# Layer 1's projections, attention and routed low-rank part as one program

## The reference

```
x = x + tanh(g_xattn[1]) * attention1(layernorm(x), ctx, Wq, Wk, Wv, Wo)     # 16 heads of 96, 4 key heads
x = x + tanh(g_ffn[1])   * lora1(layernorm(x), A, B, Wr, br)

def lora1(x, A, B, Wr, br):                       # 8 experts, rank 16
    scores = 8 * softmax(x @ Wr.T + br)           # (token, 8)
    low = einsum('bsd,hrd->bshr', x, A)           # (token, 8, 16) = 128 columns
    return 2 * einsum('bshr,hor,bsh->bso', low, B, scores)
```

## Time and profile before

| | |
|---|---|
| median of 3 runs | 2810.8 us (2809.34 to 2810.83) |
| the profiled execution, time / span | 2811.97 us / 2810.2 us |
| PE busy | 2734.7 us (97% of the span), 13880 matmuls |
| DVE, ACT, POOL busy | 1142.7, 1064.0, 664.0 us |
| granted TensorE clock, mean | 0.985 |
| stretches with PE idle of over 2 us at a time | 2371 to 2389 us and 2740 to 2764 us, and some in layer 0 |

### The profile page before, as it was taken

One profiled execution on the slowest core, in us unless ns is written; L12 is line 12 of the kernel. 1 busy time (PEld: TensorE's weight loads), 2 busy tenths in 40 slices (PEclk: granted clock), 3 DMA queues, 4 the chain that ended last, 5 costly groups with the idle time before them and its releaser, 6 DMA issues. The chain is left out here.

```text
span 2810.2 us, 37299 instructions
## 1 busy us (share of the span) xinstructions
PE 2734.7 (97%) x13880; PEld 2319.6 (83%) x13880; DVE 1142.7 (41%) x2147; ACT 1064.0 (38%) x2405; POOL 664.0 (24%) x611
## 2 busy tenths in 40 slices
PE   8999999999999998999999999999999998999997
PEld 6888888878788886888888888879899897788885
DVE  3111111122233333755666566535321010877755
ACT  4222222222233335755555555424223111755523
POOL 3000000000111112755555555403000000544410
PEclk9999999999999999999999999999999998999998
DMA  6333333332523233533333333244224221433302
GB/s 232 113 113 113 112 110 110 107 104 105 202 90 103 91 104 125 160 102 105 107 107 102 105 108 107 70 167 126 78 85 148 69 89 63 121 87 81 88 21 68
DMA packets 299883, 302.21 MB, mean 108 GB/s; under 512 B 124688, under 2 KB 252424, under 8 KB 291768
## 3 DMA queue, kind: packets, MB, share of 16 engines
q1 hardware_dynamic: 298616, 297.73, 33.7%
q10 hardware_dynamic: 1088, 2.10, 0.2%
HBM read 199.34 MB, written 100.42 MB: 107 GB/s over the span
## 5 line engine op out<-in xcount | busy, mean ns | idle before, releaser
L45 PE MATMUL pb<-p_w,p_xt 128*128 128x512 f32 (+1 forms) x992 | 397.4, 401 | 2.7 <-DVE p_w L737 2.2
L47 PE MATMUL pb<-p_w,p_xt 128*128 128x512 f32 (+1 forms) x992 | 388.9, 392 | 0.0
L46 PE MATMUL pb<-p_w,p_xt 128*128 128x512 f32 (+1 forms) x992 | 387.7, 391 | 0.0
L522 POOL TENSOR_TENSOR p_w<-p_raw,p_w 128x512 fp32r<-128x512 f32 x48 | 68.4, 1434 | 966.7 <-ACT p_w L637 966.5
L1154 ACT ACTIVATE at_p<-pb,at_nmax 112x487 f32<-112x487 f32 x256 | 171.2, 670 | 327.6 <-DVE at_nmax L1229 327.6
L745 DVE TENSOR_REDUCE p_inv<-p_sq 128x4 f32<-128x512 f32 (+1 forms) x62 | 42.6, 686 | 472.9 <-ACT p_sq L644 472.9
L45 PEld LDWEIGHTS pb<-p_w,p_xt 128*128 128x128 f32 (+1 forms) x992 | 185.4, 187 | 43.1 <-DVE p_w L737 3.1
L47 PEld LDWEIGHTS pb<-p_w,p_xt 128*128 128x128 f32 (+1 forms) x992 | 185.1, 187 | 42.5
L46 PEld LDWEIGHTS pb<-p_w,p_xt 128*128 128x128 f32 (+1 forms) x992 | 185.7, 187 | 38.2
L999 POOL TENSOR_TENSOR at_k<-at_kr,at_k 128x488 fp32r<-128x488 f32 (+1 forms) x94 | 116.2, 1236 | 365.5 <-DVE at_k L1243 365.5
L1248 DVE TENSOR_TENSOR at_ptlo<-pb,at_pthi 125x448 fp32r<-125x448 f32 (+1 forms) x256 | 148.0, 620 | 84.9 <-ACT at_pthi L1176 84.9
(11 more groups left out here) (251 smaller groups left out, 6255.1 us busy)
## 6 DMA issues: line engine op xcount, KB each, us to landing
xT_d<-p_xt SPq DMA_DIRECT2D x31, 1024.0 KB, 3.8
xc<-xT_d SPq DMA_DIRECT2D x24, 1024.0 KB, 5.5
p_raw<-in_L_xattn_Wq_dram SPq DMA_DIRECT2D x32, 512.0 KB, 4.2
at_raw<-in_L_xattn_Wo_dram SPq DMA_DIRECT2D x64, 256.0 KB, 2.8
qT_d<-p_qstage SPq DMA_DIRECT2D x56, 256.0 KB, 2.7
at_qr<-qT_d SPq DMA_DIRECT2D x64, 224.0 KB, 3.1
at_rb<-rT_d SPq DMA_DIRECT2D x64, 224.0 KB, 3.5
at_kr<-kT_d SPq DMA_DIRECT2D x64, 187.5 KB, 2.9
```

What stands on the lines that cost most here:

```text
L45: pe.matmul(out, stat_hi, mov_hi, start=start, stop=False)
L46: pe.matmul(out, stat_hi, mov_lo, start=False, stop=False)
L47: return pe.matmul(out, stat_lo, mov_hi, start=False, stop=stop)
L522: pool.tensor_tensor(w[:, 1, k, :], slab(s), f32(w[:, 0, k, :]), ALU.subtract).then_inc(w_lo_pool, 1)
```

## The change

`middle`, `attend(1, ...)` and `routed_lora` become one program, `second_layer`, in one block. Four things move.

1. In the list of events of the Q projections, `("N", i)` marks where the generators of `attend(1)` are called: SP loads the first two units' q, k and v after `("P", FS+4, 1)`; ACT, DVE cut q and k of unit 0 after `("P", FS+9, 1)`; PE makes the first two score products before `("P", FS+11, 1)` and the others behind it. Before unit 0 goes on, ACT waits until the last P product is done and its store has landed (`Room.space`), since attention's tiles lie over those of the projections.
2. A, Wr and B are turned as three more events `("G", 12)` to `("G", 14)` between P products.
3. The out-projection's last fourteen pieces use two banks instead of four (`tail_count=2`), and yield behind each second one.
4. The rest of the last stage is a chain by token tiles (`tail()`), between these pieces.

The parts of the diff that matter:

```diff
+                    if f >= 8 and f < 11:
+                        yield ("G", NF + f - 8)
+                    if f == 11:
+                        yield ("N", 0)
+                        yield ("N", 1)
                     yield ("P", FS + f, 1)
...
+                    if f == 4:
+                        yield ("N", -2)
+                    if f == 9:
+                        yield ("N", -1)
+                yield ("N", 2)
+                yield ("N", 3)
+                yield ("N", 4)
+            def tail():
+                for t in range(TT + 5):
+                    if t < TT:
+                        yield ("E", t)
+                        yield ("A", t)
+                    if 0 <= t - 4 < TT:
+                        yield ("D", t - 4)
+                    if 0 <= t - 3 < TT:
+                        yield ("L", t - 3)
+                    if 0 <= t - 2 < TT:
+                        yield ("U", t - 2)
+                        yield ("S", t - 2)
+                    if 0 <= t - 1 < TT:
+                        yield ("T", t - 1)
...
+                def space(act):
+                    act.wait_ge(p_done, 2 * (FS + NF))
+                    for p in range(2):
+                        act.wait_ge(p_stored[p], 16 * (FS + NF))
...
                 for i in range(PIECES):
-                    pe.wait_ge(added, max(first, first + i - 3))
-                    project_piece(first + i, tail_banks[i % 4])
+                    pe.wait_ge(added, max(first, first + i + 1 - tail_count))
+                    project_piece(first + i, tail_banks[i % tail_count])
+                    if i % 2:
+                        yield
...
+                        elif e[0] == "U":
+                            pe.wait_ge(x_lo, 2 * t + 2)
...
+                            for k in range(KS):
+                                last = product(pe, ub[p][:, 0:NW], lx[:, p, 0, k, :], lx[:, p, 1, k, :], wra[:, 0, k, :], wra[:, 1, k, :], k == 0, k == KS - 1)
+                        elif e[0] == "S":
+                            act.wait_ge(topped_l, t + 1)
...
+                            act.activation(expd[:, p, :], logit[:, p, :], ACT.Exp, bias=ntop[:, p:p + 1], accum_out=total[:, p:p + 1]).then_inc(exped_l, 1)
```

More of the change, by code:

```diff
@@ L121, in flamingo @@
         brb = sb(stack, "brb", [P, 8])
[L124 to L207, removed]
@@ L1372, in middle @@
             q_turned, q_hi, q_lo, p_done, p_out = (sem(f"mid_{n}") for n in ("qturn", "qhi", "qlo", "pdone", "pout"))
+            n_stats_s, n_mv_s, n_sd, n_rstd_s, n_shift_s, n_done = (sem(f"ff_{n}") for n in ("st", "mv", "sd", "rstd", "shift", "done"))
+            x_turned, x_hi, x_lo, u_done = (sem(f"ff_{n}") for n in ("xturn", "xhi", "xlo", "udone"))
+            logits, topped_l, exped_l, flipped_l, scored_l, lowered = (sem(f"ff_{n}") for n in ("logit", "top", "exp", "flip", "score", "low"))
+            low_turned, low_hi, low_lo, d_done, d_added, out_stored = (sem(f"ff_{n}") for n in ("lowturn", "lowhi", "lowlo", "ddone", "dadd", "ost"))
             def rows(i):
@@ new lines, in second_layer, with stored, finished, queries @@
+            taken = {"next": 0}
+            class Room:
+                @staticmethod
+                def stored(sp):
+                    for p in range(2):
+                        sp.wait_ge(k_stored[p], 16 * (NX // 2))
+                        sp.wait_ge(v_stored[p], 16 * ((NX + TT + 1 - p) // 2))
+                @staticmethod
+                def finished(sp):
+                    for p in range(2):
+                        sp.wait_ge(p_stored[p], 16 * (FS + NF))
+                @staticmethod
+                def queries(sp, g):
+                    for p in range(2):
+                        sp.wait_ge(p_stored[p], 16 * (FS + FS * (g + 1)))
+                @staticmethod
+                def room(pool):
+                    pool.wait_ge(v_done, NX + TT)
+                @staticmethod
+                def banks(pe):
+                    pe.wait_ge(v_out, NX + TT)
+                    pe.wait_ge(q_lo, 2 * NG)
+                @staticmethod
+                def last_banks(pe):
+                    pe.wait_ge(p_out, 2 * (FS + NF))
+                @staticmethod
+                def space(act):
+                    act.wait_ge(p_done, 2 * (FS + NF))
+                    for p in range(2):
+                        act.wait_ge(p_stored[p], 16 * (FS + NF))
@@ L1609, in columns @@
                         last.then_inc(p_done, 1)
+                    more = att.tensor(pe)
                     for e in order:
@@ L1982, in flamingo @@
         first_layer()
-        middle()
-        with ExitStack() as st:
-            def place(name, shape, dt=F32):
-                return sb(st, f"at1_{name}", shape, dt)
-            def nothing(*_):
-                return None
-            banks = [ps(st, f"at1_ps{i}", [P, BANK]) for i in range(8)]
-            run(attend(1, L1, wo1, x_sb, place, banks, Ready(*[nothing] * 6)))
-            next_stage()
-        routed_lora(x_sb)
+        second_layer()
 _INS = ["x", "ctx_4096", "g_xattn", "g_ffn", "L0_xattn_Wq", "L0_xattn_Wk", "L0_xattn_Wv", "L0_xattn_Wo",
```

393 lines of the change are left out of this document (203 added, 190 removed).

## The result

| | before | changed |
|---|---|---|
| median | 2810.24 us (4 runs) | 2775.61 us (2775.27 to 2776.32, 4 runs) |
| ratio, 95% interval | | 0.9877 (0.986 to 0.9894) |
| span of the profiled execution | 2810.2 us | 2773.5 us |
| mean granted clock | 0.985 | 0.992 |

The change saves 34.6 us; 28 were forecast (2783, range 2774 to 2797). The spans differ by 36.7 us. To see where they come from I cut both profiles at three points that PE passes in either kernel: the first matmul of layer 1's Q projections, the second unit's first score matmul, and the first of the last fourteen out-projection pieces.

What follows compares the result with a forecast made beforehand. PE, busy 97% of the span, bounds the kernel, so gains come from its idle or half-clock stretches: 10 us at attention's start plus 18 in the tail, 28 off the 2810.8 median, gives 2783 us, range 2774 to 2797.

Steps and rivals of the forecast that it cites:

- The front: Start of layer 1's attention, last P product to second unit's scores: 8.5 us instead of 18.5, 10.0 us saved.
- The price of U: In the tail, U's 24 matmuls of 136 moving columns per step: 0.11 us each, 2.6 us together.
- The step of the tail: One full step of the last stage's chain: PE 9.1 us, DVE with ACT setting it at 9.4 us.
- The drain: Tail after the last pieces are done: a chain of waits of 20.4 us, plus 2 for half clock.
- The end: After the tail's last add: 2.6 us of store landing and 0.5 to the span's end, 3.1 us.
- The signs: Profile: 3 to 4 us `at_q` wait, `mid_wra` matmuls 0.11 apart, DVE over 80% busy, add pairs 9.4 us apart.
- The sum: Whole kernel: front 10 plus tail 18, 28 us off the median of 2810.8, giving 2783 us.
- Dear small matmuls: Rival, tail: U at 24 x 0.227 = 5.4 us puts PE's step at 11.9 us; 2797 us, chance 10%.
- Table switches at twice the price: Rival, tail: each switch costs a second 1.3 us, lengthening five steps' wait for Exp; 2790 us, chance 5%.
- No gain in front: Rival: loads, cuts or store wait hold attention's unit 0 or 1 as before, only tail gains; 2793 us, chance 8%.
- A tail at half clock: Rival, slower: PE's tail step is 18.2 us instead of 9.4; 2827 us with five such steps, chance 3%.
- Two banks at no cost: Last out-projection pieces: two banks instead of four cost nothing; adds follow pieces by 0.03, next piece takes 2.04 us.

Runs made afterwards that it cites:

- front_only: Changed kernel with only the joined projections and attention; no turned blocks or tail chain, low-rank part its own stage as before: 2798.58 us, ratio to before 0.996.
- after_again: The changed kernel, unaltered, measured and profiled once more as a control: 2776.73 us.
- before_again: The kernel before, unaltered, measured and profiled once more: 2810.07 us, ratio to before 1.0001.
- u64: Changed kernel with 64 moving columns instead of 136 in the tail's matmuls for logits and low values: 2776.68 us.
- lead: Changed kernel with last-stage steps reordered: out-projection pieces up to two tiles ahead, last tile's transposes earlier in the drain; same instructions: 2770.65 us.
- the plain rule: Changed kernel with out-projection pieces of the next tile put ahead of each tile's layer norm, on PE and DVE: 2778.18 us.
- early_cut: Changed kernel with the cuts of unit 1's q and k moved ahead of unit 0's first score on ACT and DVE: 2772.62 us.
- serial_front: Changed kernel with all calls of attention's generators put behind the last P product, single block kept: 2786.32 us.

## Why the prediction was right

**The front** was right in mechanism and size. Forecast: 8.5 us beside the Q products in place of 18.5. The Q products alone are 141.6 - 18.5 = 123.1; the changed front is 131.7, so 8.6. Its parts: turning 2.3 (front_only: 129.4 against 131.7), the wait 3.49, the scores the rest. The stores and the loads of B cost nothing: PE's only wait between 2242 and 2377 us is the one of 3.49.

**The price of U**, taken as 0.11 from the transposes, came out as measured, and partly by luck: the transposes' 0.11 stands with 96 stationary columns too, so it could not show that a matmul of another number type has it.

**The step of the tail** was mis-sized, and its bound named wrongly. I had PE at 9.1, just below DVE with ACT at 9.4. PE's 9.1 was exact (9.13). That the wrong bound cost so little is luck: the two engines' steps lie within 0.4 us of each other. DVE's 9.4 is 8.7: pairs of adds take 1.40 and not 1.5, the two subtractions 1.28 and not 1.4, and in such pairs the next instruction starts before the one ahead of it has ended (2726.74 and 1.28 make 2728.02, the adds start at 2727.94), so that part of the 0.4 for hand-overs isn't there. Three full steps are 0.8 shorter for it, the two before them 0.6, the first two 0.1: 54.1 (2696.2 to 2750.3) in place of 55.7.

**The drain** was forecast 20.4 without and 22.4 with cold clock. In the changed kernel's first profile it is 20.7, from 2750.3 to the last add's end at 2771.0, with 8.6 us at 0.60. In after_again, where these run at full clock, it is some 18: 75.3 less 2.5 for the end, less 54.9. So the chain of waits is 2.5 shorter than my sum (which of its terms were too large I did not resolve), and the cold stretch costs 2.8 us where I had taken 2. Where it comes at all differs from execution to execution, so that this term came near is partly luck. The end, 3.1 forecast, is 2.5.

**The signs.** The wait of 3 to 4 us for `at_q`, the 0.11 between U's matmuls and the missing waits for a P store came as said. Two signs did not: DVE was busy for 62, 78 and 80% of the three full steps and not for over 80%, and the adds came 8.7 us apart and not 9.4. Both belong to the bound that was named wrongly. From the last piece to the end it is 28.0 us (2745.5 to 2773.5) where the prediction said some 24; that figure counts from the end of the last step (2750.3), and from there it is 23.2.

**The sum.** Front 9.9 (forecast 10) and tail 22.0 (forecast 18) in the first pair of profiles, 9.7 and 24.5 in the second (before_again, after_again). Together 31.9 to 34.2, against 34.6 in medians. So the term that was mis-sized is the tail, by 4 us in the first pair: 1.6 in the steps, 1.7 in the drain, 0.6 in the end, all on the same side, and the median lies only 0.6 us above the lower end of the stretch that got 68% (2775 to 2792). What the first pair of profiles showed beyond it, 4.8 us ahead of the Q projections, is largely chance. Over eleven profiles with layer 0 as changed this point lies between 2242.9 and 2247.9, mean 2245.6; the two of before are 2247.7 and 2246.8. The means differ by 1.6 us, and with two profiles of before against a spread of 5 us that can't be told from nothing. I did not try the wait in layer 0 alone.

**The rivals.** Dear small matmuls: refuted, 0.11, and u64 shows that below 136 the columns don't set it. Table switches at twice the price: refuted by the rows. No gain in front: refuted. A tail at half clock: full clock in all full steps; only stretches that follow waits run cold. Two banks at no cost: PE is busy for all of a full step, and none of its waits in the tail names an add; four banks with the same chain were not tried.

## What to carry to other kernels

When a chain is pipelined by tiles, the engine with the most work in a step sets it, and it is found from durations of instructions in pairs, not alone. Once the steady step is full, the time left is in the two ends: ask when the last tile's chain can begin, and move steps on every in-order engine's list, not only the busiest one's (lead gains 5 us, the plain rule loses about 2). Where two programs are joined so that the first unit starts early, prepare the second unit early as well, or the wait that stood behind the old gap remains, with a cold stretch behind it.

## What the hardware showed that was not expected

A PE wait of 3.5 us behind a dense stretch was followed by a granted clock of 0.60 to 0.79 over the next 8.3 us in every one of the profiles with it (eleven, of both kernels and their variants), and by 1.00 in the two without it; it cost 1.0 to 1.9 us more than the wait. Shorter waits did this only at times: the same instructions in the drain, 8.6 us long and with waits of 0.4 to 0.9 us ahead of them, ran at 0.60 in two profiles (changed, early_cut), at 0.80 in two (serial_front, u64) and at 1.00 in after_again. That moves a run by up to 2.8 us, as much as the smaller effects here.

With a new 128 x 128 stationary tile for each float32r matmul, 64 and 136 moving columns both take 0.11 us, 384 take 0.174 and 512 take 0.227. Transposes whose stationary tile has 128 columns but only 8 rows take 0.06.
